# Cross-attention and mixture of experts on one core: V projected in its own step, the first queries copied by VectorE, their weights on ACT's queue

## The reference

```python
q = layernorm(x) @ Wq.T + bq
k = ctx @ Wk.T + bk;  v = ctx @ Wv.T + bv
x = x + (softmax(q k^T / 4) v) @ Wo.T + bo      # per block and head
n = layernorm(x)
e = argmax(n @ wr + br)                          # one of 8 experts a token
x = x + gelu(n @ w1[e] + b1[e]) @ w2[e] + b2[e]  # 256 -> 1024 -> 256
```

## Time and profile before

| | before |
|---|---|
| median of three runs | 333.46 us (333.24 to 333.83) |
| the profiled execution | 333.26 us |
| its span, first to last instruction | 331.3 us |
| PE busy | 311.9 us (94%) |
| DVE, ACT, POOL busy | 150.4, 135.7, 157.0 us |
| first scores of step 0 start at | 10.44 us |
| mean granted clock of PE | 0.994 of full speed |

### The profile page before, as it was taken

The page is one execution under the profiler, slowest core; times in us unless marked ns, Lnnn a source line. Parts: engine busy times, 40 slices in busy tenths (PEclk is TensorE's granted clock), DMA queues, the critical chain, the costliest instruction groups (busy, mean ns, idle before and its releaser), DMA issues. The chain is left out here.

```text
span 331.3 us, 8667 instructions
## 1 busy us (share of the span) xinstructions
PE 311.9 (94%) x3061; PEld 273.5 (83%) x3061; DVE 150.4 (45%) x334; ACT 135.7 (41%) x369; POOL 157.0 (47%) x397
## 2 busy tenths in 40 slices
PE   7899999999999999878998999999999999999990
PEld 6677778888887788658897999999999999999990
DVE  2657887778778888875641111121121112112200
ACT  2565555555555565443421323342222334222220
POOL 5788667667777756685347223322222321111111
PEclk9999999999999999999999999999999999999997
DMA  5992555455400110741467864555665554555000
GB/s 156 323 348 86 162 160 160 161 160 160 160 34 34 35 36 32 269 140 41 159 239 270 300 196 178 180 185 179 247 204 191 174 195 145 161 192 193 12 0 0
DMA packets 28696, 51.84 MB, mean 156 GB/s; under 512 B 3117, under 2 KB 18607, under 8 KB 28528
## 3 DMA queue, kind: packets, MB, share of 16 engines
q1 hardware_dynamic: 24720, 43.00, 38.0%
q0 software_dynamic: 2944, 8.13, 8.7%
q10 hardware_dynamic: 992, 0.17, 0.3%
HBM read 45.01 MB, written 7.21 MB: 158 GB/s over the span
## 5 line engine op out<-in xcount | busy, mean ns | idle before, releaser
L1104 PE MATMUL scores_all<-w_sb,hT 128*128 x368 | 83.0, 379 | 0.3 <-issue 0.3
L1104 PEld LDWEIGHTS scores_all<-w_sb,hT 128*128 128x128 f32 x368 | 68.3, 190 | 9.0 <-issue 0.6
L390 POOL DMA_INDIRECT out<-y_sb,scatter_i x23 | 23.1, 1006 | 107.9 <-DVE y_sb L824 101.7
L515 ACT ACTIVATE hT<-scores_all,b_sb 128x128 f32<-128x128 f32 x96 | 27.5, 368 | 53.8 <-PE scores_all L1089 53.2
L515 ACT ACTIVATE hT<-bank,b_sb 128x128 f32<-128x128 f32 x88 | 25.3, 368 | 54.7 <-PE bank L1089 54.4
L1089 PE MATMUL scores_all<-xeT,w_slot 128*128 128x128 f32 x384 | 45.3, 275 | 0.6 <-issue 0.6
L1089 PEld LDWEIGHTS scores_all<-xeT,w_slot 128*128 128x128 f32 x384 | 44.8, 192 | 1.3 <-issue 0.8
L1089 PE MATMUL bank<-xeT,w_slot 128*128 128x128 f32 x352 | 41.6, 276 | 1.0 <-issue 0.6
L1089 PEld LDWEIGHTS bank<-xeT,w_slot 128*128 128x128 f32 x352 | 41.0, 192 | 1.7 <-issue 1.2
L809 DVE COPY xeT<-bank 128x256 f32<-128x256 f32 x20 | 8.5, 425 | 66.6 <-PE bank L1075 66.6
L625 DVE TENSOR_REDUCE peaks<-scores_all 128x16 f32<-128x2048 f32 x16 | 36.6, 2291 | 0.4 <-PE scores_all L866 0.2
(11 more groups left out here) (155 smaller groups left out, 422.9 us busy)
## 6 DMA issues: line engine op xcount, KB each, us to landing
w_slot<-in_w SPq DMA_DIRECT2D x23, 1024.0 KB, 5.7
w_sb<-in_w SPq DMA_DIRECT2D x8, 1024.0 KB, 5.8
records<-record SPq DMA_DIRECT2D x16, 256.0 KB, 2.3
gathered<-in_x SPq DMA_DIRECT2D x3, 512.0 KB, 7.8
gathered<-in_ctxT SPq DMA_DIRECT2D x3, 512.0 KB, 7.5
b_sb<-in_b SPq DMA_DIRECT2D x1, 1024.0 KB, 10.6
gathered<-records,gather_i POOLq DMA_INDIRECT x23, 4.5
out<-y_sb,scatter_i POOLq DMA_INDIRECT x23, 2.4
```

The source lines that it names most:

```text
L390: g.indirect_dma_start(out=out[:, :], out_offset=bass.IndirectOffsetOnAxis(ap=scatter_i[:, s:s + 1], axis=0), in_=y_sb[:, s % Y_RING], in_ ...
L515: ins = a.activation(hT[:, s % 2, c], H_BANK[s % 2][c // 4][:, P * (c % 4):P * (c % 4 + 1)], ACT.Gelu, bias=b1_sb[:, bass.ds(e * FC + c, 1)])
L1104: ins = t.matmul(Y_BANK[s % 2][:, 0:D], hT[:, s % 2, c], w2_flat[:, bass.ds(e * (FC * D) + c * D, D)], start=(c == 0), stop=(c == FC - 1))
```

## The change

Three things change. `wq_sb` is loaded by ACT as the first of its transfers, instead of by SP as its fourth. The first block's queries are copied from PSUM by DVE, which does this ahead of `spread_bv`; ACT only waits for it. And V of block b is projected in step b for all b, V of block 0 behind `shifted_scores(0)`, V of block 15 between `keep_busy(5)` and `shifted_scores(15)`; ACT's `take_v` moves with it.

```diff
@@ SP's loads
             load_ctx(0)
-            load_weight(wq_sb, wqT, "wq_in")
             load_x(1)
@@ ACT's loads
+            act.dma_start(wq_sb[:], wqT.rearrange("(c p) n -> p c n", p=P)).then_inc(sm["wq_in"], 16)
             act.dma_start(bk_sb[:], bkT).then_inc(sm["bk_in"], 16)
             act.dma_start(bq_sb[:], bqT).then_inc(sm["bq_in"], 16)
@@ ACT, ahead of the steps
             take_k(0)
             act.wait_ge(sm["bq_in"], 16)
-            take_q(0)
-            act.wait_ge(sm["consts_pool"], 3)
-            take_v(0)
+            act.wait_ge(sm["q_taken"], 1)
             take_xT(1)
@@ ACT, step b
                 if live(b + 1) and b > 0:
                     take_k(b + 1)
-                    take_v(b + 1)
+                if b > 0:
+                    take_v(b)
                 exps(b)
                 if b == 0:
-                    take_v(1)
+                    act.wait_ge(sm["consts_pool"], 3)
+                    take_v(0)
                     take_xT(2)
@@ DVE, ahead of the steps
             stats_x(1)
+            dve.wait_ge(sm["bq_in"], 16)
+            dve.wait_ge(sm["q_ready"], 1)
+            for c in range(KC):
+                ins = v.tensor_scalar(q_whole[:, 0, c], V_BANK[:, P * c:P * (c + 1)], bq_sb[:, c:c + 1], None, ALU.add)
+            ins.then_inc(sm["q_taken"], 1)
             spread_bv()
@@ PE, route(b)
                 wait_for(pe, "q_taken", b + 5)
+                wait_for(pe, "v_taken", b + 3)
@@ PE, project_v(b)
-                wait_for(pe, "q_taken", b + 1)
-                wait_for(pe, "logits_taken", b - 3)
-                if b == FIRST + 4:
+                wait_for(pe, "q_taken", b + 2)
+                wait_for(pe, "logits_taken", b - 2)
+                if b == NB - 1:
+                    pe.wait_ge(sm["ids_taken"], 1)
+                if b == FIRST + 3:
                     pe.wait_ge(sm["rank_saved"], 1)
@@ PE, project_q(b)
-                wait_for(pe, "v_taken", b)
+                wait_for(pe, "v_taken", b - 1)
@@ PE, name_tokens(0)
-                    pe.wait_ge(sm["v_taken"], NB)
+                    pe.wait_ge(sm["v_taken"], NB - 1)
@@ PE, step b
                 if b == 0:
-                    project_v(0)
                     turn_x(1)
...
                     keep_busy(5)
                 if b == 0:
                     project_q(1)
-                elif live(b + 1):
-                    project_v(b + 1)
+                else:
+                    project_v(b)
                 shifted_scores(b)
                 if b == 0:
-                    project_v(1)
+                    project_v(0)
```

## The result

| | before | after |
|---|---|---|
| median of 20 executions | 333.84 us | 335.76 us |
| fastest and slowest of them | 333.24, 334.82 us | 334.48, 337.29 us |
| the profiled execution, and its span | 333.26, 331.3 us | 335.89, 334.2 us |
| turned maxima of step 0 start | 14.07 us | 15.60 us |
| turned maxima of step 0 to those of step 15 | 128.14 us | 128.16 us |

The ratio is 1.0053 (95% interval 1.0040 to 1.0066): the change makes the kernel slower by half a per cent. The forecast was 333.6, 0.15 us over the 333.46 of three runs, with a range that ended at 334.6, and a chance of 0.20 for slower; the medians now lie 1.92 us apart. One of the changed kernel's executions took 1559 us, which is a disturbance: the ratio and the slowest execution leave it out, and the median would be 335.75 without it.

What follows compares the result with a forecast made beforehand. TensorE was taken as busy throughout except at two edges, the first 12 us and step 15. A 0.2 us gain at the start and 0.35 us loss in step 15 gave +0.15, about 333.6 us, range 332.8 to 334.6.

Steps and rivals of the forecast that it cites:

- The start's compute chain: Block 0: Q follows K without waiting, DVE copies q in 0.65 us; first scores at 9.95, 0.49 us gained, other things equal.
- the remark that K would then be last: Block 0 copies: at an estimated 0.26 us per DVE copy, q would be 0.13 us earlier and k ready last.
- (a): Start: x(0) shares bandwidth with Q's weights and lands 0 to 0.36 us late, taken as 0.25, with no cover.
- (b): Start: ctx(0), landing at 6.13, is delayed 0.73 or 1.8 us by Q's weights; the first taken, hidden before K.
- (c): Start: small loads bk_sb and bq_sb stand behind Q's weights on ACT's queue; even 2 us of delay are hidden.
- (d): Start: bv_col, behind Q's weights, lands between 9.87 and 12.1, taken as 10.4; the first maximum can start from 11.4.
- (e): Start: bytes ahead of x(2) unchanged in sum, so it lands at 10.88 at the latest; maximum from 11.5.
- R1: Rival, start: bv_col stuck behind Q's weights holds DVE; landing at 11.5 loses 0.8 us there, 334.6 us total; chance 0.20.
- V(15): Step 15 gains one V projection: some 0.35 us lost, between 0 and 0.6; shifted scores start 0.54 us late.
- R2: Rival, step 15: the added V projection is hidden as in steps 1 to 14, giving 333.3 us; chance 0.14.
- A difference in clock is not what moves this kernel: Whole kernel: TensorE's clock is at its upper level, 2.4 GHz, in all profile slices but the last.
- steps 1 to 14: Middle attention steps: V of the next block replaced by the step's own V in the same position, cost 0.

Runs made afterwards that it cites:

- best: Kernel before with q(0) by VectorE, small loads late, bv spread behind first maximum, WARM = 22, six fillers before step 15's turned maxima: 333.16 us, ratio 0.9976.
- wq_act_only: Kernel before with only Q's weights moved to the head of ACT's queue: 334.71 us against 333.56, ratio 1.0032.
- after_bv_late: Changed kernel with the spreading of bv on VectorE moved behind the first maximum: 334.86 us against 333.86 for the kernel before, ratio 1.0032.
- after_bv_late_warm23: Changed kernel with bv spread behind the first maximum and 23 instead of 20 warm-up transposes: 334.08 us against 333.86 for the kernel before, ratio 0.9999.
- after_fill0: Changed kernel with seven filler transposes in step 0 where V of block 0 stood: 334.67 us against 333.82 for the kernel before, ratio 1.0030.
- after_small_late: Changed kernel with ACT's four small loads issued by SP behind context group 2, bv spread behind first maximum: 333.54 us against 333.82 before, ratio 1.0002.

## Why the prediction was wrong

1. *The start's compute chain* was right as far as it went: where nothing else was late (best), K at 7.13, Q 0.90 us behind it, a DVE pair of 0.61 us (forecast 0.65), and the first scores at 9.95, to the hundredth as forecast. That is luck in part: Q followed K 0.16 us sooner than counted, while K was 0.09 us later and the scores started 0.15 us behind the copy instead of 0.05. The single copy took 0.35 us, not the estimate of 0.26; and with that estimate q would have been there at 9.77, still behind k at 9.71, so the remark that K would then be last is wrong.
2. *x(0)* (a): forecast 0.25 us late, measured 0.32 in the changed kernel, 0.43 in two others, over the bound of 0.36. ctx(0) (b) and the small bk, bq (c) were hidden, as said.
3. *The failed step is (d) with (e).* They gave 0.2 us gained at the start; where K and Q kept their pace (wq_act_only) the maximum came 1.10 us later. (d) took 10.4 us for `bv_col`, on the ground that the engines are only 0.56 busy between 4 and 7 us and so have room. They have not: ACT's four small loads keep them at that rate (without them 303 GB/s), and with 262 KB more in front of them the poor stretch lasted until 9 us. `bv_col` came at 12.24, just over the bound of 12.1. (e) took equal bytes for an equal landing and gave 10.88 "at the latest"; x group 2 came at 12.03. That was a bound without a row for the rate. The Trainium skill's rule that I weighed there ("DMA: Bandwidth & Descriptors", "Issuing engines are not separate DMA queues": both queues end on the same 16 engines and interleave) agrees with x(0), `bv_col` and x group 2 all coming later. R1 named the mechanism and its bound, landing + 0.99: 13.23 against the measured 13.27, an agreement that half-pace K and Q would have given too; in wq_act_only the maximum starts 0.76 us behind `spread_bv`. It had 0.20.
4. *V(15)* was forecast at 0.35 us. At full clock it is 0.03 (after_bv_late): `shifted_scores(15)` starts 0.38 later and not 0.54 (1.78 us behind the turned maxima instead of 1.40), since V starts 0.54 us behind the first of the five fillers, where the sum had the 0.71 of their row; the wait ahead of `project_o(14)` takes up 0.25 of it, where the sum had 0.18, so that it starts 0.13 later, and it is 0.10 shorter (1.03 instead of 1.13). R2 was nearer. Where the clock fell, the same distance was 1.65 us longer, but 0.7 to 1.3 us of that kind a fall costs without V(15) too.
5. *"A difference in clock is not what moves this kernel"* failed too: the sum put the clock at nothing. One profile with the clock up in all slices was taken for all executions, and about half of those of the kernel before are not like it. How the 1.92 us between the medians divide is not settled. 1.24 stand between the fastest executions too, but in other kernels with Q's weights at the head of ACT's queue and the small loads in their old place it is 0.34 (after_bv_late_warm23) to 1.17 (after_fill0). What is shown is that the queue costs at the start (1.10 us in wq_act_only's profile; gone in after_small_late), and that a fall of the clock costs 0.7 to 1.65 us in step 15, or 1.5 to 1.65 between the turned maxima of steps 0 and 15 where it comes in step 0. Falls in step 0 stand in 2 of 10 profiles with the new V order, behind idle times of 1.55 and 2.01 us, and in none of 7 with the old one; whether taking V(0) out of step 0 makes them come stays open.
6. The distance between the turned maxima of steps 0 and 15 did not change (128.14 and 128.16), as steps 1 to 14 said. For a start that gains, though, that step of the forecast would have failed: in the eight profiles whose turned maxima of step 0 start between 13.57 and 14.26 us, with no fall and no loss before step 15, those of step 15 start between 142.21 and 142.45, in no order with the first (the next one, 14.33, has 142.73). The 0.2 us would hardly have been seen at the end. What takes such a gain up was not looked for.

## What to carry to other kernels

A transfer moved to the head of another queue delays what was first there and all that the same DMA engines serve; look for the smallest transfer behind it for which an engine waits that works in order, and for what stands behind that wait. Engines half busy in the profile of the start need not be room for more bytes: find what keeps them slow and move that away (here four small loads, 174 to 303 GB/s). A profile is one execution: when the time of a kernel scatters, look at the mean clock of all executions before a profile is called typical and before a loss in it is put down to the edit; here the kernel before has the same fall as the changed one. And follow a gain at the start to the last step before it is counted.

## What the runs showed of the hardware

The granted clock fell to 0.50 over stretches of more than 3 us, in step 0 or step 15, in some executions of the same kernel and not in others; with it eight matmuls of 128 columns took 1.92 us instead of 1.06. The idle time ahead of the turned maxima of step 15 was 1.15 us with a fall (9 profiles) and without (6), and 0.45 us in two without; in step 0 it was 1.55 and 2.01 us with a fall, and at most 1.42 without. The Trainium skill ("TensorE: Matmul & The Clock Gate", "HAM oscillation") says that TensorE comes back at its lower clock from an idle gap that is long enough. Idle time stood ahead of every fall here, but the same 1.15 us with and without a fall show that the length of this gap alone does not decide it. Four small loads (a broadcast of 128 KB, and 4, 32 and 1 KB in pieces down to 4 bytes) held the DMA engines to 149 to 178 GB/s for 3 to 5 us at a busy share of 0.56 to 0.68; with the four issued later it was 303 GB/s at 1.00. Which of the four does it was not tried.
